# Attention over heads: GpSimd adds the halves of the weighted values of ten heads; the sum, the spread and the output each get a slot of their own

## The chip, the cores and the metric

The kernel runs on one core of a Trainium2 chip. The metric is device time in microseconds of one execution. Before the change three runs took 3179.53, 3181.57 and 3188.43 us (median 3181.57). The engines are called as in the profile: PE (TensorE, with PEld for its weight loads), DVE (VectorE), ACT (ScalarE), POOL (GpSimd) and SP (SyncE).

## The reference, cut to what matters

The program is a decoder of two layers with six parts, on 64 batches of 128 tokens with 128 features in float32. The changed part is the fourth, attention over heads: each token attends, within itself, from each of its 16 heads to each of its 16 heads; a head has 8 features.

```python
def _L1_attn_ref(x, Wq, Wk, Wv, Wo, bo):
    N_HEADS = 16
    N, S, D = x.shape
    H = N_HEADS
    hd = D // H
    q = (x @ Wq.T).reshape(N, S, H, hd).transpose(0, 2, 1, 3)
    k = (x @ Wk.T).reshape(N, S, H, hd).transpose(0, 2, 1, 3)
    v = (x @ Wv.T).reshape(N, S, H, hd).transpose(0, 2, 1, 3)
    att = jnp.einsum('nqhd,nkhd->nhqk', q, k)
    att = jax.nn.softmax(att / jnp.sqrt(jnp.asarray(hd, x.dtype)), axis=3)
    out = jnp.einsum('nhqk,nkhd->nqhd', att, v).reshape(N, S, D)
    return out @ Wo.T + bo
...
x = x + _L1_attn_ref(_layernorm(x, axis=-1), L1_attn_Wq, ...)
```

After the transpose q, k and v are (batch, head, token, feature), while the einsum reads its letters as if token stood before head: so the softmax runs over pairs of heads, separately for each token. The result, (batch, head, token, feature of the head), is reshaped to 128 rows of 128 without a transpose: row 8 h + t // 16 of the output comes from head h and the sixteen tokens of group t // 16. In the kernel a token is a partition, and the scores of one token are a 16 x 16 square in the free dimension.

## The kernel before, in words

The kernel runs its parts one after the other, each as a stage with a barrier at its end. The whole `x` (128 partitions of tokens, 64 batches, 128 features) stays in SBUF. The changed stage is `attention_over_heads`, lines 1455 to 1626. It handles one batch at a time, in a pipeline written out by hand. Time is cut into slots; `run_slots` (lines 52 to 64) gives each engine its own instructions for slot after slot, the first and last slots written out, the middle ones in a loop unrolled by four. In slot t a step with lag n works on batch t - n. There is no planner: an engine carries out the steps in the order in which its function lists them, and waits on semaphores before each.

The steps of one batch, with their lags before the change:

- lag 0 and `TURN` (1): ACT normalizes into `xn` (L1544), PE transposes it (L1515), ACT copies it to `xT` (L1538), POOL adds the output bias to `x` (L1580).
- `PROJECT` (2): PE computes q, k and v (L1520), ACT copies them to `qkv` (L1550).
- `MULTIPLY` (3): POOL multiplies q and k of all 16 x 16 pairs of heads into `qk`, 2048 elements per token (L1575).
- `SCORE` (4): PE adds up the eight features with sixteen matmul instructions against the identity (L1508); DVE takes the maximum (L1613) and subtracts it (L1616); ACT takes the exponential into `ps_e` (L1564).
- `WEIGH` (5): DVE multiplies the weights with v into `ev`, 2048 elements per token (L1597), sums the weights (L1599), takes the reciprocal (L1601), sums `ev` over its last 16 (L1603) and scales to `o` (L1607).
- `SPREAD` (6): ACT writes `o` eight times into `r`, each time scaled by the mask of one group of sixteen tokens (L1557).
- `LAST` (7): PE multiplies with the output weights (L1526), DVE adds to `x` (L1622) and takes statistics (L1624). One slot later, for every fourth batch, POOL computes the scalars of the next normalization for four batches (`scalars_of_four`, lines 171 to 246), a chain of small instructions each of which waits for the one before.

Within a slot the order on each engine is: PE scores, transpose, projection, output; ACT `xT`, `xn`, `qkv`, spread, exponential; POOL `qk`, bias, scalars; DVE weigh (all five instructions), maximum and difference, addition to `x` and statistics. `qkv` has four buffers, `qk`, `dif`, `o`, `r` and `ps_e` two, `ev`, `z` and `rz` one.

Of the kernel before, what the change touches and what calls it, by code (L numbers as in the profile page):

```python
# [18 lines left out]
ALU = mybir.AluOpType  # L19
ACT = mybir.ActivationFunctionType  # L20
AX = mybir.AxisListType

P = 128
D = 128
HEADS = 16
HD = 8
# [40 lines left out]
def wait(eng, sem, value):  # L67

    if not (isinstance(value, int) and value <= 0):
        eng.wait_ge(sem, value)  # L70
# [1384 lines left out]
def attention_over_heads(c):  # L1455
# [3 lines left out]

    nc, B = c.nc, c.B  # L1460
    A = P // HEADS
    ctx, sb, ps, sem = stage_scope(c)
    with ctx:
        xn, xT = sb("xn", [P, 2, D]), sb("xT", [P, 2, P])
        qkv = sb("qkv", [P, UNROLL, 3, HD, HEADS])
        qk = sb("qk", [P, 2, HD, HEADS, HEADS])
        top, dif = sb("top", [P, HEADS]), sb("dif", [P, 2, HEADS, HEADS])
        z, rz = sb("z", [P, HEADS]), sb("rz", [P, HEADS])
        ev = sb("ev", [P, HEADS, HD, HEADS])
        o = sb("o", [P, 2, HEADS, HD])  # L1470
        r = sb("r", [P, 2, HD, HEADS, A])
        ps_x, ps_qkv, ps_y = ps("ps_x"), ps("ps_qkv"), ps("ps_y")
        ps_s = [ps(f"ps_s{i}") for i in range(2)]
        ps_e = [ps(f"ps_e{i}") for i in range(2)]
        names = ("xn_ready", "xT_ps", "xT_ready", "qkv_ps", "qkv_ready", "qk_ready", "s_ps", "top_done", "dif_ready", "exp_done",
                 "z_done", "rz_done", "ev_done", "sums_done", "o_ready", "r_ready", "y_ps", "x_done", "biased")
        (xn_ready, xT_ps, xT_ready, qkv_ps, qkv_ready, qk_ready, s_ps, top_done, dif_ready, exp_done,
         z_done, rz_done, ev_done, sums_done, o_ready, r_ready, y_ps, x_done, biased) = (sem(n) for n in names)
        block = ctx.enter_context(nc.Block())

        TURN, PROJECT, MULTIPLY, SCORE, WEIGH, SPREAD, LAST = 1, 2, 3, 4, 5, 6, 7
        LAG = LAST
        full = [P, HD, HEADS, HEADS]
        final_in = sem("final_in")
# [9 lines left out]
        def weights_of(u):  # L1494
            return ps_e[u % 2][:, 0:HEADS * HEADS].rearrange("p (i j) -> p i j", i=HEADS)

        def sums_of(u):
            return ps_e[u % 2][:, HEADS * HEADS:HEADS * HEADS + D].rearrange("p (i d) -> p i d", i=HEADS)

        @block.tensor  # L1500
        def _(pe):
# [29 lines left out]
        @block.scalar  # L1531
        def _(act):
            def slot(sl):
                if at := sl.step(TURN):
                    s, u = at
                    act.wait_ge(xT_ps, s + 1)
                    wait(act, qkv_ps, s - 1)
                    nc.scalar.activation(xT[:, u % 2, :], ps_x[:, 0:P], ACT.Copy).then_inc(xT_ready, 1)  # L1538
                if at := sl.step(0):
                    s, u = at  # L1540
                    wait(act, xT_ps, s - 1)
                    if sl.fixed and sl.t == MULTIPLY + 1:
                        act.wait_ge(late_rated, 4)
                    nc.scalar.activation(xn[:, u % 2, :], c.x[:, s, :], ACT.Identity, scale=c.rstd[:, bass.ds(s, 1)],  # L1544
                                         bias=c.shift[:, bass.ds(s, 1)]).then_inc(xn_ready, 1)
                if at := sl.step(PROJECT):
                    s, u = at
                    act.wait_ge(qkv_ps, s + 1)
                    wait(act, ev_done, s - 3)
                    nc.scalar.activation(qkv[:, u, :, :, :], ps_qkv[:, 0:3 * D].rearrange("p (n d h) -> p n d h", n=3, h=HEADS),  # L1550
                                         ACT.Copy).then_inc(qkv_ready, 1)
                if at := sl.step(SPREAD):
                    s, u = at
                    act.wait_ge(o_ready, s + 1)
                    wait(act, y_ps, s - 1)
                    for a in range(A):
                        ins = nc.scalar.activation(r[:, u % 2, :, :, a], o[:, u % 2, :, :].rearrange("p h d -> p d h"), ACT.Copy,  # L1557
                                                   scale=c.w["a1_rows"][:, a:a + 1])
                    ins.then_inc(r_ready, 1)
                if at := sl.step(SCORE):  # L1560
                    s, u = at
                    act.wait_ge(dif_ready, s + 1)
                    wait(act, o_ready, s - 1)
                    nc.scalar.activation(weights_of(u), dif[:, u % 2, :, :], ACT.Exp, scale=HD ** -0.5).then_inc(exp_done, 1)  # L1564

            run_slots(act, slot, B, LAG)

        @block.gpsimd
        def _(pool):
            def slot(sl):  # L1570
                if at := sl.step(MULTIPLY):
                    s, u = at
                    pool.wait_ge(qkv_ready, s + 1)
                    wait(pool, s_ps, s - 1)
                    nc.gpsimd.tensor_tensor(qk[:, u % 2, :, :, :], qkv[:, u, 0, :, :].unsqueeze(3).broadcast_to(full),  # L1575
                                            qkv[:, u, 1, :, :].unsqueeze(2).broadcast_to(full), ALU.mult).then_inc(qk_ready, 1)
                if at := sl.step(TURN):
                    s, u = at
                    pool.wait_ge(xn_ready, s + 1)
                    nc.gpsimd.tensor_tensor(c.x[:, s, :], c.x[:, s, :], c.w["a1_b"][:, :], ALU.add).then_inc(biased, 1)  # L1580
                if sl.fixed and sl.t == MULTIPLY:
                    scalars_of_four(c, pool, late_scaled, late_rated, B - 4, four, False, True, 0)
                if (at := sl.step(LAST + 1)) and at[1] % 4 == 3 and not (sl.fixed and at[0] == B - 1):
                    s, u = at
                    pool.wait_ge(stats_done, s + 1)
                    scalars_of_four(c, pool, scaled, rated, s - 3, four, False, True)

            run_slots(pool, slot, B, LAG)

        @block.vector  # L1590
        def _(dve):
            def slot(sl):
                if at := sl.step(WEIGH):
                    s, u = at
                    n = [P, HEADS, HD, HEADS]
                    dve.wait_ge(exp_done, s + 1)
                    nc.vector.tensor_tensor(ev[:, :, :, :], weights_of(u).unsqueeze(2).broadcast_to(n),  # L1597
                                            qkv[:, u, 2, :, :].unsqueeze(1).broadcast_to(n), ALU.mult).then_inc(ev_done, 1)
                    nc.vector.tensor_reduce(z[:, :], weights_of(u), AX.X, ALU.add).then_inc(z_done, 1)  # L1599
                    dve.wait_ge(z_done, s + 1)  # L1600
                    nc.vector.reciprocal(rz[:, :], z[:, :]).then_inc(rz_done, 1)  # L1601
                    dve.wait_ge(ev_done, s + 1)
                    nc.vector.tensor_reduce(sums_of(u), ev[:, :, :, :], AX.X, ALU.add).then_inc(sums_done, 1)  # L1603
                    dve.wait_ge(rz_done, s + 1)
                    dve.wait_ge(sums_done, s + 1)
                    wait(dve, r_ready, s - 1)
                    nc.vector.tensor_tensor(o[:, u % 2, :, :], sums_of(u), rz[:, :].unsqueeze(2).broadcast_to([P, HEADS, HD]),  # L1607
                                            ALU.mult).then_inc(o_ready, 1)
                if at := sl.step(SCORE):
                    s, u = at  # L1610
                    dve.wait_ge(s_ps, s + 1)
                    score = ps_s[u % 2][:, 0:HEADS * HEADS].rearrange("p (i j) -> p i j", i=HEADS)
                    nc.vector.tensor_reduce(top[:, :], score, AX.X, ALU.max).then_inc(top_done, 1)  # L1613
                    dve.wait_ge(top_done, s + 1)
                    wait(dve, exp_done, s - 1)
                    nc.vector.tensor_tensor(dif[:, u % 2, :, :], score, top[:, :].unsqueeze(2).broadcast_to([P, HEADS, HEADS]),  # L1616
                                            ALU.subtract).then_inc(dif_ready, 1)
                if at := sl.step(LAST):
                    s, u = at
                    dve.wait_ge(y_ps, s + 1)  # L1620
                    dve.wait_ge(biased, s + 1)
                    nc.vector.tensor_tensor(c.x[:, s, :], c.x[:, s, :], ps_y[:, 0:D], ALU.add).then_inc(x_done, 1)  # L1622
                    dve.wait_ge(x_done, s + 1)
                    nc.vector.bn_stats(c.stats[:, s, :], c.x[:, s, :]).then_inc(stats_done, 1)  # L1624

            run_slots(dve, slot, B, LAG)


# [1109 lines left out]
```

## Time and profile before

| what | value |
|---|---|
| median of three runs | 3181.57 us |
| profiled execution, its own time | 3173.24 us |
| profiled execution, span of the core | 3171.5 us |
| mean granted TensorE clock over the span | 0.958 |
| busy over the span: PE, PEld, DVE, ACT, POOL | 89%, 73%, 70%, 60%, 57% |
| first `ev` to last `ev` start (64 batches) | 1737.3 to 2169.7 us |

The rows below come from one profiled execution. Rows in order of time show the start and the duration of an instruction or of a run of equal ones ("x16" is sixteen of them), and in brackets the idle time of the engine before it and what ended it. A start-to-start distance can be shorter than a duration, because an engine takes up its next instruction before the last one's end is recorded. Rows of groups show the number of instructions, the busy time of all, and the mean duration in ns.

### The profile page before, as it was taken

How to read it: one execution, taken by the hardware profiler on the slowest of the kernel's cores; microseconds unless marked ns; L12 is line 12 of the kernel's file. 1: busy time of each engine (PE TensorE's matmuls, PEld its weight loads, DVE VectorE, ACT ScalarE, POOL GpSimd, SP SyncE). 2: the span in 40 equal slices, each digit the busy share in tenths (PEclk: the TensorE clock that was granted, in tenths of full speed). 3: DMA queues.
4: the chain of work that ended last, by engine and by line, in shares of the span. 5: the costliest groups of instructions: out<-in, count | busy, mean ns of one | idle time of the engine just before them, and what ended most of it. 6: DMA issues, size and time to landing. Idle time of an engine off the chain costs nothing. (4 is left out here: it accounts for less than half of the span.)

```text
span 3171.5 us, 79074 instructions
## 1 busy us (share of the span) xinstructions
PE 2810.4 (89%) x26182; PEld 2315.9 (73%) x26183; DVE 2213.5 (70%) x4747; ACT 1914.9 (60%) x4303; POOL 1819.8 (57%) x2990
## 2 busy tenths in 40 slices
PE   6999997999999999499995999996789999999996
PEld 4666675888888888387774777774467777777775
DVE  4877885667666676445553999996878787878643
ACT  2555553666666666354442667674677777777762
POOL 3333333556666666425556777773667777777752
PEclk9999998999999999699997999997699999999998
DMA  5555563000000000122222000000000000000000
GB/s 151 156 143 157 157 169 107 2 5 13 14 11 13 13 12 15 68 69 74 74 74 68 1 0 0 0 0 1 1 1 5 8 5 8 5 8 5 8 5 10
DMA packets 205118, 129.51 MB, mean 41 GB/s; under 512 B 14256, under 2 KB 197528, under 8 KB 204184
## 3 DMA queue, kind: packets, MB, share of 16 engines
q1 hardware_dynamic: 196632, 108.60, 12.1%
q0 software_dynamic: 8192, 16.79, 1.7%
q8 instruction: 208, 3.41, 0.4%
q14 instruction: 86, 0.70, 0.1%
HBM read 34.85 MB, written 90.51 MB: 40 GB/s over the span
## 5 line engine op out<-in xcount | busy, mean ns | idle before, releaser
L445 ACT ACTIVATE a_e<-a_ps_s 128x512 f32<-128x512 f32 x256 | 138.9, 595 | 216.9 <-PE a_ps_s L371 216.9
L1575 POOL TENSOR_TENSOR a_qk<-a_qkv 128x2048 f32<-128x2048 f32 x64 | 235.3, 3676 | 57.8 <-ACT a_qkv L1550 53.6
L1508 PE MATMUL a_ps_s<-a_qk,w_ident 128*128 128x256 f32 x1024 | 236.7, 385 | 26.5 <-POOL a_qk L1575 26.4
L988 POOL TENSOR_TENSOR x_p<-x_p,x_rz 128x1232 f32<-128x1232 f32 x64 | 143.9, 2248 | 170.4 <-DVE x_rz L1097 170.4
L1508 PEld LDWEIGHTS a_ps_s<-a_qk,w_ident 128*128 128x128 f32 x1024 | 192.1, 192 | 55.9 <-issue 22.4
L524 POOL TENSOR_TENSOR a_k_bd<-a_kT,w_block 128x512 f32<-128x512 f32 x64 | 67.1, 1050 | 280.2 <-ACT a_kT L476 280.2
L1366 POOL DMA_INDIRECT f_yg<-f_rows_out,f_index x128 | 122.8, 959 | 177.7 <-DVE f_yo L1446 159.3
L547 DVE TENSOR_REDUCE a_nmax<-a_ps_s 128x4 f32<-128x512 f32 x256 | 164.0, 682 | 84.3 <-PE a_ps_s L366 84.3
L1557 ACT ACTIVATE a_r<-a_o,w_a_rows 128x128 f32<-128x128 f32 x512 | 220.8, 522 | 2.1 <-DVE a_o L1607 2.1
L2224 POOL TENSOR_TENSOR x_sq<-x_e 128x1232 f32<-128x1232 f32 x64 | 143.3, 2240 | 127.4 <-DVE x_t_sq L2383 127.3
L1104 DVE TENSOR_REDUCE x_top<-x_ps_s 128x16 f32<-128x1232 f32 x64 | 91.2, 1425 | 110.3 <-PE x_ps_s L728 110.3
L2102 ACT ACTIVATE x_pT<-x_ps_s 77x512 f32<-77x512 f32 x256 | 142.3, 590 | 34.6 <-PE x_ps_s L1979 34.6
L1526 PEld LDWEIGHTS a_ps_y<-w_a_o,a_r 128*128 128x128 f32 x1024 | 123.1, 195 | 54.6 <-issue 36.3
L865 ACT ACTIVATE x_uu_hi<-x_ps_u 128x308 fp32r<-128x308 f32 x256 | 101.7, 423 | 90.6 <-PE x_ps_u L728 90.4
L366 PE MATMUL a_ps_s<-a_k_bd,a_q 32*128 32x128 f32 x2048 | 154.1, 289 | 1.2 <-issue 1.2
L2205 POOL TENSOR_TENSOR x_d<-x_d,x_g 128x1232 f32<-128x1232 f32 x64 | 144.0, 2249 | 18.5 <-ACT x_g L2164 18.5
L1526 PE MATMUL a_ps_y<-w_a_o,a_r 128*128 128x128 f32 x1024 | 131.4, 283 | 24.4 <-DVE x L1622 24.2
L1979 PE MATMUL x_ps_s<-w_ident,x_d 128*77 128x128 f32 x1024 | 145.2, 280 | 7.7 <-DVE x_d L2366 7.6
L1597 DVE TENSOR_TENSOR a_ev<-a_ps_e,a_qkv 128x2048 f32<-128x2048 f32 x64 | 146.0, 2281 | 5.2 <-ACT a_ps_e L1564 4.1
L882 ACT ACTIVATE x_pT<-x_ps_s 77x512 f32<-77x512 f32 x256 | 140.0, 594 | 13.4 <-PE x_ps_s L786 12.0
L1979 PEld LDWEIGHTS x_ps_s<-w_ident,x_d 128*77 128x77 f32 x1024 | 124.4, 152 | 31.2 <-issue 22.1
L1019 POOL DMA_INDIRECT f_rows_in<-f_xr,f_where x120 | 121.1, 1009 | 39.2 <-issue 28.6
(588 smaller groups left out, 9755.6 us busy)
## 6 DMA issues: line engine op xcount, KB each, us to landing
f_rows_in<-a_zeros SPq DMA_DIRECT2D x31, 1088.0 KB, 5.4
f_rows_out<-a_zeros SPq DMA_DIRECT2D x31, 1088.0 KB, 10.2
f_xin<-f_rows_in SPq DMA_DIRECT2D x135, 64.0 KB
f_rows_out<-f_yo SPq DMA_DIRECT2D x135, 64.0 KB
out<-x SPq DMA_DIRECT2D x16, 256.0 KB
f_raw<-in_late_f SPq DMA_DIRECT2D x2, 1408.0 KB, 6.1
w_ctx<-in_ctx SPq DMA_DIRECT2D x1, 2464.0 KB
f_rows_in<-f_xr,f_where POOLq DMA_INDIRECT x128
```

What stands on the lines that cost most here:

```text
L366: nat = nc.tensor.matmul(ps_s[g][:, j * P:j * P + P], q[strip(g), u % 4, :], k_bd[strip(g), u % 4, j, :], start=False, stop=j == GROUP - 1)
L547: nc.vector.tensor_reduce(nmax[:, g, :], ps_s[g][:, :].rearrange("p (t k) -> p t k", t=GROUP), AX.X, ALU.max, negate=True).then_inc(max_do ...
L988: nc.gpsimd.tensor_tensor(wide, wide, rz[:, :].unsqueeze(2).broadcast_to([P, HEADS, K]), ALU.mult).then_inc(p_ready, 1)
L1508: ins = nc.tensor.matmul(ps_s[u % 2][:, 0:HEADS * HEADS], c.ident[:, :], qk[:, u % 2, k, :, :], start=k == 0, stop=k == HD - 1)
L1526: ins = nc.tensor.matmul(ps_y[:, 0:D], r[:, u % 2, k, :, :], c.w["a1_o"][:, k, :], start=k == 0, stop=k == HD - 1)
L1557: ins = nc.scalar.activation(r[:, u % 2, :, :, a], o[:, u % 2, :, :].rearrange("p h d -> p d h"), ACT.Copy, scale=c.w["a1_rows"][:, a:a + 1])
L1575: nc.gpsimd.tensor_tensor(qk[:, u % 2, :, :, :], qkv[:, u, 0, :, :].unsqueeze(3).broadcast_to(full), qkv[:, u, 1, :, :].unsqueeze(2).broad ...
L1597: nc.vector.tensor_tensor(ev[:, :, :, :], weights_of(u).unsqueeze(2).broadcast_to(n), qkv[:, u, 2, :, :].unsqueeze(1).broadcast_to(n), ALU ...
L1979: ins = nc.tensor.transpose(ps_s[0:K, r, j * P:j * P + P], d[:, spread % RING, r, j, :], c.ident[:, :])
L2102: nc.scalar.activation(pT[:, GROUP * r:GROUP * r + GROUP, :], ps_s[0:K, r, :].rearrange("p (j q) -> p j q", j=GROUP), ACT.Copy).then_inc(p ...
L2205: nc.gpsimd.tensor_tensor(wide, wide, g[:, a, b, :].unsqueeze(2).broadcast_to([P, HEADS, K]), ALU.mult).then_inc(dg_ready, 1)
L2224: nc.gpsimd.tensor_tensor(sq[:, :, :], e[:, s % 2, :, :], e[:, s % 2, :, :], ALU.mult).then_inc(sq_ready, 1)
```

## The change

POOL adds, for the first ten heads, the upper eight of each sixteen weighted values to the lower eight, into a new tile `pairs` (640 elements per token). DVE sums the sixteen values for the other six heads, and the eight pair sums for these ten. `WEIGH` is cut in two: the product, the sum of the weights and the reciprocal stay in it; the sums and `o` go to a new step `SUM`, one slot later. `SPREAD` and `LAST` go one slot later too. `ev` and `rz` get two buffers, the sums a PSUM bank of their own. ACT's exponential waits for `ev` and `z` of the batch before instead of `o`. In POOL's order the new add stands between the `qk` product and the bias addition; DVE does `SUM` between `WEIGH` and the maximum.

```diff
+    HALF, FOLDED = HEADS // 2, 10
...
-        z, rz = sb("z", [P, HEADS]), sb("rz", [P, HEADS])
-        ev = sb("ev", [P, HEADS, HD, HEADS])
+        z, rz = sb("z", [P, HEADS]), sb("rz", [P, 2, HEADS])
+        ev = sb("ev", [P, 2, HEADS, HD, HEADS])
+        pairs = sb("pairs", [P, 2, FOLDED, HD, HALF])
...
+        ps_sums = ps("ps_sums")
...
-        TURN, PROJECT, MULTIPLY, SCORE, WEIGH, SPREAD, LAST = 1, 2, 3, 4, 5, 6, 7
+        TURN, PROJECT, MULTIPLY, SCORE, WEIGH, SUM, SPREAD, LAST = 1, 2, 3, 4, 5, 6, 7, 8
...
-        def sums_of(u):
-            return ps_e[u % 2][:, HEADS * HEADS:HEADS * HEADS + D].rearrange("p (i d) -> p i d", i=HEADS)
+        sums = ps_sums[:, 0:D].rearrange("p (i d) -> p i d", i=HEADS)
...
                     act.wait_ge(dif_ready, s + 1)
-                    wait(act, o_ready, s - 1)
+                    wait(act, ev_done, s - 1)
+                    wait(act, z_done, s - 1)
...
+                if at := sl.step(WEIGH):
+                    s, u = at
+                    pool.wait_ge(ev_done, s + 1)
+                    wait(pool, sums_done, 2 * (s - 1))
+                    nc.gpsimd.tensor_tensor(pairs[:, u % 2, :, :, :], ev[:, u % 2, 0:FOLDED, :, 0:HALF], ev[:, u % 2, 0:FOLDED, :, HALF:HEADS],
+                                            ALU.add).then_inc(paired, 1)
...
                     dve.wait_ge(exp_done, s + 1)
-                    nc.vector.tensor_tensor(ev[:, :, :, :], weights_of(u).unsqueeze(2).broadcast_to(n),
+                    wait(dve, paired, s - 1)
+                    nc.vector.tensor_tensor(ev[:, u % 2, :, :, :], weights_of(u).unsqueeze(2).broadcast_to(n),
...
-                    nc.vector.reciprocal(rz[:, :], z[:, :]).then_inc(rz_done, 1)
+                    nc.vector.reciprocal(rz[:, u % 2, :], z[:, :]).then_inc(rz_done, 1)
+                if at := sl.step(SUM):
+                    s, u = at
                     dve.wait_ge(ev_done, s + 1)
-                    nc.vector.tensor_reduce(sums_of(u), ev[:, :, :, :], AX.X, ALU.add).then_inc(sums_done, 1)
+                    nc.vector.tensor_reduce(sums[:, FOLDED:HEADS, :], ev[:, u % 2, FOLDED:HEADS, :, :], AX.X, ALU.add).then_inc(sums_done, 1)
+                    dve.wait_ge(paired, s + 1)
+                    nc.vector.tensor_reduce(sums[:, 0:FOLDED, :], pairs[:, u % 2, :, :, :], AX.X, ALU.add).then_inc(sums_done, 1)
                     dve.wait_ge(rz_done, s + 1)
-                    dve.wait_ge(sums_done, s + 1)
+                    dve.wait_ge(sums_done, 2 * (s + 1))
                     wait(dve, r_ready, s - 1)
-                    nc.vector.tensor_tensor(o[:, u % 2, :, :], sums_of(u), rz[:, :].unsqueeze(2).broadcast_to([P, HEADS, HD]),
+                    nc.vector.tensor_tensor(o[:, u % 2, :, :], sums, rz[:, u % 2, :].unsqueeze(2).broadcast_to([P, HEADS, HD]),
                                             ALU.mult).then_inc(o_ready, 1)
```

## Rows read from the trace of the kernel before

**Rows 1.** The page: busy time, share of the span and instructions of each engine.
```profile
PE 2810.4 (89%) x26182; PEld 2315.9 (73%) x26183; DVE 2213.5 (70%) x4747; ACT 1914.9 (60%) x4303; POOL 1819.8 (57%) x2990
```
**Rows 2.** Busy time by stretch, the stage's middle; after the engines PEclk, DMA, GB/s.
```profile
1900.00:2000.00 100.00, 91.84 (x518) 77.20 (x517) 94.48 (x133) 68.79 (x174) 72.82 (x81) 1.00 0.00 0
```
**Rows 3.** Order of time, DVE, one batch: start, duration, engine, line, operation.
```profile
2012.84 2.27 DVE L1597 TENSOR_TENSOR a_ev<-a_ps_e,a_qkv 128x2048 f32<-128x2048 f32 x1
2015.03 0.41 DVE L1599 TENSOR_REDUCE a_z<-a_ps_e 128x16 f32<-128x256 f32 x1
...
2015.65 2.24 DVE L1603 TENSOR_REDUCE a_ps_e<-a_ev 128x128 f32<-128x2048 f32 x1
2017.98 0.29 DVE L1607 TENSOR_TENSOR a_o<-a_ps_e,a_rz 128x128 f32<-128x128 f32 x1
...
2019.61 2.27 DVE L1597 TENSOR_TENSOR a_ev<-a_ps_e,a_qkv 128x2048 f32<-128x2048 f32 x1
```
**Rows 4.** Order of time, POOL, around one chain of scalars.
```profile
1971.86 0.20 POOL L207 TENSOR_TENSOR a_four<-stats 128x4 f32 x1 [2.15 <-DVE stats L1624]
...
1977.78 3.67 POOL L1575 TENSOR_TENSOR a_qk<-a_qkv 128x2048 f32<-128x2048 f32 x1 [0.32 <-issue]
...
1981.41 0.45 POOL L1580 TENSOR_TENSOR x<-x,w_a_b 128x128 f32 x1
...
1981.83 3.67 POOL L1575 TENSOR_TENSOR a_qk<-a_qkv 128x2048 f32<-128x2048 f32 x1
```
**Rows 5.** Order of time, PE, around the scores behind a chain.
```profile
1954.14 3.72 PE L1508 MATMUL a_ps_s<-a_qk,w_ident 128*128 128x256 f32 x16 [1.58 <-POOL a_qk L1575]
...
1981.58 3.71 PE L1508 MATMUL a_ps_s<-a_qk,w_ident 128*128 128x256 f32 x16 [1.57 <-POOL a_qk L1575]
...
1985.24 0.81 PE L1520 MATMUL a_ps_qkv<-w_a_qkv,a_xT 128*128 128x384 f32 x2
...
1987.67 3.62 PE L1508 MATMUL a_ps_s<-a_qk,w_ident 128*128 128x256 f32 x16
```
**Rows 6.** Groups by line and shape, POOL, whole span: count, busy, mean ns.
```profile
L524 POOL TENSOR_TENSOR a_k_bd<-a_kT,w_block 128x512 f32<-128x512 f32 x64 | 67.1, 1050 | 280.2 <-ACT a_kT L476 280.2
...
L2232 POOL TENSOR_TENSOR x_full<-x_full,f_row_f2b 128x512 f32<-128x512 f32 x16 | 20.3, 1268 | 1.3
...
L975 POOL COPY x_raw<-w_ctx 128x308 f32 x10 | 4.5, 452 | 0.0
```
**Rows 7.** Order of time, ACT, in the slot behind a chain.
```profile
1986.17 0.49 ACT L1550 ACTIVATE a_qkv<-a_ps_qkv 128x384 f32<-128x384 f32 x1
1986.56 3.46 ACT L1557 ACTIVATE a_r<-a_o,w_a_rows 128x128 f32<-128x128 f32 x8
```
**Rows 8.** Order of time, all engines: an exponential and the `ev` behind it.
```profile
1964.20 0.39 ACT L1564 ACTIVATE a_ps_e<-a_dif 128x256 f32<-128x256 f32 x1 [1.64 <-DVE a_dif L1616]
...
1964.72 2.27 DVE L1597 TENSOR_TENSOR a_ev<-a_ps_e,a_qkv 128x2048 f32<-128x2048 f32 x1
```
**Rows 9.** Order of time, PE, matmuls behind idle time, at the stage's ends.
```profile
1738.20 5.41 PE L1508 MATMUL a_ps_s<-a_qk,w_ident 128*128 128x256 f32 x16 [3.19 <-POOL a_qk L1575]
...
2162.85 2.02 PE L1526 MATMUL a_ps_y<-w_a_o,a_r 128*128 128x128 f32 x16 [1.21 <-DVE x L1622]
2169.54 3.49 PE L1526 MATMUL a_ps_y<-w_a_o,a_r 128*128 128x128 f32 x16 [4.67 <-DVE x L1622]
2175.44 3.21 PE L1526 MATMUL a_ps_y<-w_a_o,a_r 128*128 128x128 f32 x16 [2.41 <-DVE x L1622]
```
**Rows 10.** Busy time by stretch, one microsecond within the first of these.
```profile
1740.00:1741.00 1.00, 1.00 (x4) 0.77 (x3) 1.00 (x2) 0.00 (x0) 1.00 (x1) 0.50 0.00 0
```
**Rows 11.** Order of time, DVE: first `ev`, last `ev`, last instruction of the stage.
```profile
1737.27 2.29 DVE L1597 TENSOR_TENSOR a_ev<-a_ps_e,a_qkv 128x2048 f32<-128x2048 f32 x1 [2.09 <-ACT a_ps_e L1564]
...
2169.65 2.29 DVE L1597 TENSOR_TENSOR a_ev<-a_ps_e,a_qkv 128x2048 f32<-128x2048 f32 x1
...
2181.66 0.29 DVE L1624 BATCH_NORM_STATS2 stats<-x 128x6 f32<-128x128 f32 x1
```

More of the change, by code:

```diff
@@ L1474, in attention_over_heads @@
         ps_e = [ps(f"ps_e{i}") for i in range(2)]
-        names = ("xn_ready", "xT_ps", "xT_ready", "qkv_ps", "qkv_ready", "qk_ready", "s_ps", "top_done", "dif_ready", "exp_done",
+        ps_sums = ps("ps_sums")
+        names = ("paired", "xn_ready", "xT_ps", "xT_ready", "qkv_ps", "qkv_ready", "qk_ready", "s_ps", "top_done", "dif_ready", "exp_done",
                  "z_done", "rz_done", "ev_done", "sums_done", "o_ready", "r_ready", "y_ps", "x_done", "biased")
-        (xn_ready, xT_ps, xT_ready, qkv_ps, qkv_ready, qk_ready, s_ps, top_done, dif_ready, exp_done,
+        (paired, xn_ready, xT_ps, xT_ready, qkv_ps, qkv_ready, qk_ready, s_ps, top_done, dif_ready, exp_done,
          z_done, rz_done, ev_done, sums_done, o_ready, r_ready, y_ps, x_done, biased) = (sem(n) for n in names)
         block = ctx.enter_context(nc.Block())
-        TURN, PROJECT, MULTIPLY, SCORE, WEIGH, SPREAD, LAST = 1, 2, 3, 4, 5, 6, 7
+        TURN, PROJECT, MULTIPLY, SCORE, WEIGH, SUM, SPREAD, LAST = 1, 2, 3, 4, 5, 6, 7, 8
         LAG = LAST
```

## The prediction

> **What bounds the kernel now.** I read the engine totals first: no engine is full over the whole span (PE 89%, DVE 70%, POOL 57%) [rows 1], so the changed stage has to be read by itself. It is attention over heads, from about 1725 to 2182 us. In the table by stretch its middle shows DVE busy 94.5 of 100 us, PE 91.8, POOL 72.8, ACT 68.8, with TensorE at its full clock [rows 2]. DVE bounds it. Next I read DVE in order of time: one batch from `ev` to the next `ev` takes 2019.61 - 2012.84 = 6.77 us without a gap, 2.33 us of it the sum over 16 values (start of the sum to start of `o`) [rows 3]. Then GpSimd: every fourth slot it runs the chain of small instructions for the scalars of four batches (5.92 us from L207 to the next `qk`); a `qk` and the bias add take 4.05 us together [rows 4]. Last PE: the score matmuls that come behind that chain start 27.44 us after their predecessors four slots before [rows 5]. So the beat of the stage is four slots in 27.44 us, 4 x 6.77 = 27.1 of them DVE.
>
> **The change, part by part.** *What DVE loses.* The one sum of 2048 elements becomes one of 768 (six heads) and one of 640 (ten heads, already halved). From the sums of 2048 in 2.24 us and of 256 in 0.41 us an element costs 1.02 ns and an instruction about 0.15 [rows 3]: 0.93 + 0.80 = 1.73 instead of 2.24, so DVE's slot falls to about 6.2 us. That is a gain only if nothing else sets the beat.
>
> *What GpSimd gains.* One add per batch, 64 in all, 640 elements with two different inputs. No row has 640. The nearest is the add of 512 elements with two full inputs, 1268 ns; the bias add of 128 took 0.45 [rows 4, 6]. That is 2.12 ns an element, so 1.54 us, or 1.50 to the start of the next. Bounds: the product with one broadcast operand, 512 in 1.05 us [rows 6], gives 1.30; the copy with one input, 308 in 0.45 us, scaled to 640 gives 0.94; the upper end is 1.75, if each element cost a sixth more than the dearest row. I take 1.50, by the nearest row (an add with two full inputs).
> GpSimd's needs in four slots before: 4 x 4.05 + 5.92 = 22.1 us, so it has 5.3 us free of 27.44. Four adds need 6.0. **The cover is too small**: by its own work alone the beat becomes 28.1 us. Part of its spare time is a wait of 2.15 us for the statistics before L207 [rows 4]; the rest it waits for `qkv`.
> The Trainium skill, Perfetto Trace Analysis, "GPSIMD Engine Instruction", says that a GpSimd span in a profile isn't to be relied on and should be timed from start to start. By that the add is 1.50 and not 1.54, which over 64 is under 3 us; the sum above goes by starts already.
>
> *The wait that it adds.* GpSimd's order in a slot is `qk`, add, bias add, and at every fourth the chain. The add waits for `ev` of the same slot, and behind it in the queue stand the chain and the next `qk`, for which PE's scores wait. Let a `qk` behind a chain end at 0. From there, in this kernel's rows: scores start at 0.13 (1981.45 to 1981.58); PE works a whole slot, 6.09 (1981.58 to 1987.67); from the next scores to the end of the projection 4.47 (1981.58 to 1986.05) [rows 5]; ACT copies `qkv` and starts the spread after 0.12 + 0.39, and the eight spread instructions take 3.46 [rows 7]. `exp` is queued behind them, 0.39, then 0.13 until `ev` starts [rows 8], and 2.28 until it ends [rows 3]. Sum 17.46 us: that is when the add of the third slot on can start. GpSimd by its own work would be there at 3 x (1.50 + 0.41 + 3.63) = 16.6. It waits 0.8 us, and then: add 1.50, bias 0.41, chain 5.92, `qk` 3.67. The beat is 17.46 + 11.50 = **28.96 us**. With the add at 0.94 this loop would still give 28.4.
>
> *What becomes of PE.* Its four slots take 4 x 6.09 = 24.4 us, and all of its idle time falls in one piece, in front of the scores behind the chain: 4.5 us instead of 1.57 [rows 5]. What such a hole does is to be seen at the stage's ends [rows 9]. After an idle 3.19 us sixteen score matmuls took 5.41 us instead of 3.62 [rows 5]; after 4.67 and 2.41 us the sixteen output matmuls took 3.49 and 3.21 instead of 2.02 after 1.21. The granted clock was 0.50 in such a piece (1.2 instead of 2.4 GHz) [rows 10]. After 1.57 us nothing of the kind is seen [rows 5]. So I expect the clock to fall once per beat, at a price of 1.2 to 1.8 us; I take 1.5. The scores so slowed stand at the head of the loop above, so the price is paid in full: **30.46 us** a beat.
> The Trainium skill, TensorE: Matmul & The Clock Gate, "Why this matters for your kernels", warns of TensorE idle gaps between bursts, after which the clock goes back to half. The rows above agree. If the rule did not bite here, the beat would stay at 28.96 us.
>
> *Two buffers, `rz` by two, own bank, exp's new waits.* `exp` now waits for `ev` and `z` of the batch before, both over when DVE has made its `dif`: nothing. The second `ev` buffer and the separate PSUM bank cost no instruction; at most they lengthen no wait. *One slot more of lag*: below, at the end.
>
> **The sum**, against the profiled execution (span 3171.5). First `ev` at 1737.3 as before [rows 11]. GpSimd isn't yet full in the seven slots up to the first chain in the loop (slots 5 to 12): PE's pace of 6.1 and 2 us of start, so `ev` of slot 12 at 1782. Its end, add, bias, chain, `qk`: + 2.3 + 1.5 + 0.4 + 5.9 + 3.7 = 1796. There are 14 chains (slots 12 to 64), so 13 full beats: 13 x 30.46 = 396, 2192. From there to the last `ev`: add 1.5, then PE's and DVE's last slots, 11.1 by DVE's pace, and once more 1.5 for the clock: 14.1, 2206. From the last `ev` to the end of the last statistics 12.3 us before [rows 11]; now the wait for the add and the slot more put two spreads (7 us) one behind the other: 15.2. End of the stage 2221.3 instead of 2182.0 [rows 11]: **+39.3 us**. What follows the stage (fed by a barrier) is unchanged. The span becomes 3210.8. The profiled execution took 3173.2 by its own time, the median shown is 3181.57, 8.3 above it; the difference put on the median gives **3221**.
>
> **Rivals.**
> *B, the clock holds.* Same loop, but TensorE stays at full clock through a 4.5 us hole. For it: in the stage's middle the clock never left 1.00 [rows 2]. Against: three holes out of three of 2.4 us and more were followed by slow matmuls [rows 9]. 14 x 1.5 = 21 less: +18.3, 3200.
> *C, GpSimd's work alone.* The add finds `ev` ready always, the clock fall is absorbed. Beat 28.1: 13 x 0.86 less than B: +7, 3189. Against: `exp` is queued behind the spread [rows 7, 8], which I can't see shortened. This is also the most that a cheap add can make of the loop (0.94 gives a beat of 28.4).
> *D, faster.* One mechanism: GpSimd does the adds in the time that it now idles in front of L1575 and L207. It decides where four adds fit 5.3 us, at 1.33 us an add, and where `ev` is early enough not to be waited for. At 0.94 GpSimd would need 25.9 a beat, against 4 x 6.2 = 24.8 of DVE: 13 x 1.6 = 21 less, and 5 less at the ends: 3155. For it: the products with a broadcast operand are that cheap or nearly. Against: every add with two full inputs is dearer, and the loop.
> *E, dearer.* The add at 1.75 and register work of the added waits showing in the chain: 14 x 1.3 = 18 more, 3239.
>
> **How the numbers follow.** Own case 0.57, with its range 3208 to 3232 (the price of the clock, 14 x 0.3 either way, and of the add, 14 x 0.25 x 1 up or down, and a few us between runs). B 0.17, C 0.11, D 0.08, E 0.07. The range reaches down to C's middle and up to just short of E: 3187 to 3235, leaving out D, half of C and most of E. A measurement of this kernel can tell 0.3%, 9.5 us, from no change. Slower by more: own case, B, E and a share of C, 0.82; within: 0.10; faster: D, 0.08.
>
> **What would show it.** Right: POOL above 90% busy in the stage's middle, DVE near 85%; `pairs` add about 1.5 us; a wait of GpSimd for `ev` once in four slots; scores behind a chain 30 us apart, idle over 4 us before them, 5.2 us long instead of 3.7, and granted clock about 0.9 in the stage. The two sums 0.93 and 0.80 us. Wrong: the add under 1.3 us; beats under 28; the clock at 1.00 in the stage (then B or C); DVE still above 90%.

## The result, and the profile after

| kernel | median, us | runs |
|---|---|---|
| before | 3180.55 | 4 |
| after | 3226.86 | 4 |
| ratio | 1.0138, 95% interval 1.0113 to 1.0164 | |

The kernel became slower by 1.38%, 36 to 52 us; 3221 was forecast. The profiled execution took 3228.11 us, span 3226.3, 54.8 longer than before. From the first `ev` to the first matmul of the next stage the changed stage took 486.3 us (1749.63 to 2235.95), before 445.6 (1737.27 to 2182.85): **+40.7**, and +39.3 was forecast. The part ahead of the stage, whose code is the same, was 12.4 us longer in this execution (over the profiles of the experiments the first `ev` starts anywhere from 1712 to 1747 us), the part behind it 1.7. So I compare stages by their own length, and programs by the ratios of medians.

Busy time by engine over the span, after; the counterpart before is in [rows 1]:
```profile
PE 2840.5 (88%) x26182; PEld 2350.6 (73%) x26183; DVE 2179.5 (68%) x4811; ACT 1922.2 (60%) x4303; POOL 1918.5 (59%) x3054
```
Here the reader sees nearly nothing: DVE gave up 34 us, POOL took on 99, and PE, whose work didn't change, is busy 30 us longer. The stage's middle, by stretch as in [rows 2] (behind the five engines stand the granted TensorE clock, DMA, GB/s):
```profile
1900.00:2000.00 100.00, 86.63 (x459) 74.29 (x458) 74.85 (x128) 61.25 (x154) 86.09 (x90) 0.90 0.00 0
```
DVE went from 94.5 to 74.9 us of 100, POOL from 72.8 to 86.1, and no engine is full. A beat that got longer with no engine full is a loop of waits, or work that is slow while it counts as busy; here it is both. What the changed instructions cost, after, in groups (count, busy, mean ns, idle time before them and what ended it), and who waits for whom in the stage (us in total, times, longest):
```profile
L1510 PE MATMUL a_ps_s<-a_qk,w_ident 128*128 128x256 f32 x1024 | 265.7, 419 | 68.4 <-POOL a_qk L1578 68.4
L1607 DVE TENSOR_TENSOR a_ev<-a_ps_e,a_qkv 128x2048 f32<-128x2048 f32 x64 | 146.2, 2284 | 26.5 <-ACT a_ps_e L1567 24.1 <-issue 2.4
L1584 POOL TENSOR_TENSOR a_pairs<-a_ev 128x640 f32<-128x640 f32 x64 | 98.4, 1538 | 48.8 <-DVE a_ev L1607 48.8
L1615 DVE TENSOR_REDUCE a_ps_sums<-a_ev 128x48 f32<-128x768 f32 x64 | 57.8, 903 | 0.0
L1617 DVE TENSOR_REDUCE a_ps_sums<-a_pairs 128x80 f32<-128x640 f32 x64 | 51.9, 811 | 0.0
```
```profile
PE a_ps_s L1510 <- POOL a_qk L1578: 54.0, 12, 4.9
POOL a_pairs L1584 <- DVE a_ev L1607: 32.5, 22, 2.3
```
The add is 1.54 us and the sums 0.90 and 0.81: the prices are as forecast (1.54, 0.93, 0.80). PE waits twelve times, 4.5 us each, for the `qk` behind a chain. In order of time, PE's score matmuls (start, duration, idle before and what ended it), to be set beside [rows 5]:
```profile
1929.10 5.96 PE L1510 MATMUL a_ps_s<-a_qk,w_ident 128*128 128x256 f32 x16 [4.46 <-POOL a_qk L1578]
1937.44 3.62 PE L1510 MATMUL a_ps_s<-a_qk,w_ident 128*128 128x256 f32 x16
...
1960.05 5.85 PE L1510 MATMUL a_ps_s<-a_qk,w_ident 128*128 128x256 f32 x16 [4.46 <-POOL a_qk L1578]
...
1990.89 5.41 PE L1510 MATMUL a_ps_s<-a_qk,w_ident 128*128 128x256 f32 x16 [4.46 <-POOL a_qk L1578]
...
2021.28 5.95 PE L1510 MATMUL a_ps_s<-a_qk,w_ident 128*128 128x256 f32 x16 [4.46 <-POOL a_qk L1578]
```
The beats are 30.95, 30.84 and 30.39 us, and the short one is the one that begins with the short scores (5.41). POOL in order of time through one beat, to be set beside [rows 4]:
```profile
1956.33 3.67 POOL L1578 TENSOR_TENSOR a_qk<-a_qkv 128x2048 f32<-128x2048 f32 x1
...
1967.38 3.67 POOL L1578 TENSOR_TENSOR a_qk<-a_qkv 128x2048 f32<-128x2048 f32 x1
1973.27 1.56 POOL L1584 TENSOR_TENSOR a_pairs<-a_ev 128x640 f32<-128x640 f32 x1 [2.22 <-DVE a_ev L1607]
...
1979.67 1.55 POOL L1584 TENSOR_TENSOR a_pairs<-a_ev 128x640 f32<-128x640 f32 x1 [0.79 <-DVE a_ev L1607]
1981.17 0.46 POOL L1589 TENSOR_TENSOR x<-x,w_a_b 128x128 f32 x1
1981.58 0.21 POOL L207 TENSOR_TENSOR a_four<-stats 128x4 f32 x1
...
1987.16 3.67 POOL L1578 TENSOR_TENSOR a_qk<-a_qkv 128x2048 f32<-128x2048 f32 x1
```
POOL waits for `ev` in the third and fourth slot of the beat, then does add, bias, chain and `qk` one behind the other (11.16 us from 1979.67 to the end of `qk`), while PE waits. The granted clock around the hole (the hole, the first 4 us of scores, the 2 us after):
```profile
1955.50:1960.00 4.50, 0.09 (x1) 0.00 (x0) 4.29 (x8) 2.62 (x7) 4.18 (x5) 0.73 0.00 0
1960.00:1962.00 2.00, 1.95 (x5) 1.59 (x6) 1.97 (x4) 0.00 (x0) 2.00 (x3) 0.50 0.00 0
1962.00:1964.00 2.00, 2.00 (x6) 1.60 (x5) 1.41 (x3) 0.00 (x0) 2.00 (x1) 0.50 0.00 0
1964.00:1966.00 2.00, 2.00 (x10) 1.69 (x9) 0.07 (x1) 0.00 (x0) 2.00 (x2) 0.90 0.00 0
```
The clock falls inside the hole and stays at 0.50, 1.2 GHz, for the first four microseconds of scores: 5 or 6 matmuls in 2 us, against 10 and more later.

### The profile page after: what moved, and what is told of

Same layout as the page of the kernel before. It is cut to its first block and busy times, and to the rows that moved or that the text cites. A ratio compares the mean times of both kernels' runs of the same rounds, so it can differ in the third digit from the quotient of the medians.

```text
span 3226.3 us, 79417 instructions
## 1 busy us (share of the span) xinstructions
PE 2840.5 (88%) x26182; PEld 2350.6 (73%) x26183; DVE 2179.5 (68%) x4811; ACT 1922.2 (60%) x4303; POOL 1918.5 (59%) x3054
## 5 line engine op out<-in xcount | busy, mean ns | idle before, releaser
L1510 PE MATMUL a_ps_s<-a_qk,w_ident 128*128 128x256 f32 x1024 | 265.7, 419 | 68.4 <-POOL a_qk L1578 68.4
L1510 PEld LDWEIGHTS a_ps_s<-a_qk,w_ident 128*128 128x128 f32 x1024 | 212.5, 213 | 106.9 <-POOL a_qk L1578 74.2
L1019 POOL DMA_INDIRECT f_rows_in<-f_xr,f_where x120 | 121.4, 1012 | 39.0 <-issue 28.1
L1305 PE MATMUL f_ps_y<-f_w,f_aT 128*128 x810 | 123.0, 289 | 22.8 <-DVE f_yo L1446 19.7
```

The source lines that it names most:

```text
L1510: ins = nc.tensor.matmul(ps_s[u % 2][:, 0:HEADS * HEADS], c.ident[:, :], qk[:, u % 2, k, :, :], start=k == 0, stop=k == HD - 1)
```

## The experiments

My theory after the result: the new wait for `ev` of the same slot, with the chain behind it in POOL's queue, closes a loop of 28.7 us, and the clock fall adds about 2.2 us to it. Rivals: POOL's work alone (C), and the clock as a consequence that costs nothing. Ratios are to the kernel before in runs on the same chip, with 95% intervals; "stage" is first `ev` to the next stage's first matmul, set against 445.6; it is of the one profiled execution, which can lie some us off the median. A beat is four slots, scores behind a chain to the next such scores.

### The add alone, without and with its wait

The kernel before, with one more POOL add of 640 elements per batch, on a tile of ones (`still`) that nothing else touches; DVE's work is unchanged. The second kernel has the marked line too.
```diff
+                if at := sl.step(WEIGH):
+                    s, u = at
+                    wait(pool, padded, s - 1)
+                    pool.wait_ge(ev_done, s + 1)      # the second kernel only
+                    nc.gpsimd.tensor_tensor(pairs[:, u % 2, :, :, :], still[:, :, :, 0:HEADS // 2], still[:, :, :, HEADS // 2:HEADS], ALU.add).then_inc(padded, 1)
```
Without the wait:

> The kernel before, with an add of 640 elements of a constant tile in every slot of GpSimd, in the place of the new add, its result unused; it waits for nothing of DVE's. Theory (most of the loss is the wait for ev and what it sets off): GpSimd's own work makes the beat 28.1 us, so +5 to +24 us, about 3190, with GpSimd never waiting for DVE in mid-stage. Rival (the load of the add on GpSimd by itself is the loss): as slow as the changed kernel, 3220 or more.

With the wait:

> As the one with the constant add, but the add waits for ev of its slot, as the new add does; DVE still sums all 2048 elements. Theory: the loop closes, with DVE's longer slot (6.77 instead of 6.2 us) in it: beat about 31.6 us, +50 us, about 3234, so at least 25 us slower than the one without the wait. Rival (the load alone): the same time as without the wait, within 8 us.

Measured without it: ratio 1.0030 (1.0018 to 1.0042), 3188.39 us, stage 454.6, +9.0; a beat of 28.1. With it: 1.0191 (1.0169 to 1.0214), 3237.51 us, stage 503.4, +57.8. The times are as expected (about 3190 and 3234). PE's scores behind the chain, without the wait:
```profile
1910.79 5.40 PE L1511 MATMUL a_ps_s<-a_qk,w_ident 128*128 128x256 f32 x16 [3.84 <-POOL a_qk L1581]
1938.85 5.40 PE L1511 MATMUL a_ps_s<-a_qk,w_ident 128*128 128x256 f32 x16 [2.13 <-POOL a_qk L1581]
1966.93 3.72 PE L1511 MATMUL a_ps_s<-a_qk,w_ident 128*128 128x256 f32 x16 [2.14 <-POOL a_qk L1581]
1995.03 3.72 PE L1511 MATMUL a_ps_s<-a_qk,w_ident 128*128 128x256 f32 x16 [3.04 <-POOL a_qk L1581]
```
The reader sees slow and full-clock scores, and the same beat of 28.06 to 28.10 behind either: while POOL's own work bounds the stage, the clock fall is free. With the wait, of what POOL waited for:
```profile
POOL a_pairs L1587 <- DVE a_ev L1608: 31.8, 20, 2.3
```
The wait with what it sets off, the fall of the clock included, and not the add's 1.5 us, makes +49 of the +58. Here DVE still has its whole sum in the slot, so this loop is longer than that of the changed kernel.

### The clock kept up

The changed kernel, with extra matmuls into columns of PSUM that nobody reads, in the last slot of the beat: the hole is filled, the loop stays. First 13 calls, then 9.
```diff
+                    if u == 1:
+                        pe.wait_ge(xT_ready, min(s + LAST, B) if sl.fixed else s + LAST)
+                        for _ in range(13):      # 9 in the second kernel
+                            nc.tensor.matmul(ps_x[:, P:3 * P], c.ident[:, :], c.w["a1_qkv"][:, 0:2 * P], start=True, stop=True)
```
13 calls:

> The changed kernel, with 13 more matmuls of 256 columns on PE behind the output matmuls of the slot after each chain of scalars, into columns of PSUM that nobody reads (work that the result doesn't need). They fill about 3 of the 4.5 us in which PE waits for the products. Theory (wait loop and clock): the clock stays at 1.00, the scores behind a chain take 3.7 us again instead of 5.4 to 6.2, the beat of four slots falls from 30.9 to about 28.9 us, the time by 14 x 2.1 = 29 us to about 3198. Rival (the clock fall is absorbed somewhere, GpSimd's work or its wait alone makes the time): less than 5 us off the changed kernel's 3227.

9 calls:

> As the kernel with 13 added matmuls, with 9 of them: 13 ran 5.8 us and held the scores behind them back by 1.06 us in each beat (29.6 us a beat, clock 1.00); 9 should run 4.0 us and end before the products are there. Theory (wait loop, and the clock's price on it): clock 1.00, beat 28.5 to 29.0 us, 14 x 2.1 = 29 us off the changed kernel: about 3198. Rival (the 9 us that 13 matmuls gained were all there is to the clock): 3217.

13 calls: 1.0113 (1.0090 to 1.0137), 3217.53 us, stage 481.2. That missed (3198 was expected): the fillers took 5.78 us, not 3, and overran the hole. Each call is two matmuls in the trace (x26), where I had reckoned with one. `qk` ended at 1955.79, the scores started 1.06 later:
```profile
1951.24 5.78 PE L1533 MATMUL a_ps_x<-w_a_qkv,w_ident 128*128 128x256 f32 x26
...
1952.12 3.67 POOL L1582 TENSOR_TENSOR a_qk<-a_qkv 128x2048 f32<-128x2048 f32 x1
...
1956.85 3.62 PE L1510 MATMUL a_ps_s<-a_qk,w_ident 128*128 128x256 f32 x16
```
9 calls: 1.0055 (1.0036 to 1.0073), 3167.47 us against 3148.08, +19.4; stage 464.5, +18.9; rival B gave +18.3 for a kept clock. PE, the window, and POOL's one wait of the beat:
```profile
1922.23 3.72 PE L1510 MATMUL a_ps_s<-a_qk,w_ident 128*128 128x256 f32 x16 [0.56 <-POOL a_qk L1582]
1950.92 3.72 PE L1510 MATMUL a_ps_s<-a_qk,w_ident 128*128 128x256 f32 x16 [0.55 <-POOL a_qk L1582]
```
```profile
1900.00:2000.00 100.00, 98.35 (x555) 85.49 (x554) 83.02 (x140) 69.12 (x173) 91.13 (x97) 1.00 0.00 0
```
```profile
1939.73 1.55 POOL L1588 TENSOR_TENSOR a_pairs<-a_ev 128x640 f32<-128x640 f32 x1 [0.80 <-DVE a_ev L1611]
```
Clock 1.00, beat 28.69, one wait of 0.80 us: this is the loop of the prediction (28.96, one wait of 0.8) laid bare. With it the beats of the changed kernel come out within 0.02 us: scores of 5.41 instead of 3.72 give 28.69 + 1.69 = 30.38 (measured 30.39), of 5.96 give 30.93 (30.95), of 5.85 give 30.82 (30.84). The clock's part is thus shown: 486.3 - 464.5 = 22 us of the stage, from one profiled execution of each, on different chips.

### A short add in the same place

`FOLDED` 2 instead of 10 in the changed kernel: POOL's load nearly as before, the waits the same, DVE's sums longer.
```diff
-    HALF, FOLDED = HEADS // 2, 10
+    HALF, FOLDED = HEADS // 2, 2
```

> The changed kernel with 2 heads folded instead of 10: the add is 128 elements (0.45 instead of 1.54 us), DVE sums 14 heads over 16. GpSimd's own work is then 23.7 us a beat, under the 27.4 of before. Theory (the wait for ev with the chain behind it closes the loop whatever the add costs): beat 30.9 - 1.1 (add) + 0.4 (DVE's longer slot) = 30.2 us, clock still falling, about 3216. Rival (GpSimd's load is the cause): no slower than before, 3180 or less.

Measured 1.0145 (1.0117 to 1.0174), 3194.90 us against 3148.08, +46.8; stage 489.2.
```profile
1924.12 6.30 PE L1510 MATMUL a_ps_s<-a_qk,w_ident 128*128 128x256 f32 x16 [3.88 <-POOL a_qk L1578]
1954.83 6.31 PE L1510 MATMUL a_ps_s<-a_qk,w_ident 128*128 128x256 f32 x16 [3.88 <-POOL a_qk L1578]
```
```profile
1900.00:2000.00 100.00, 88.36 (x471) 75.93 (x470) 82.14 (x128) 64.00 (x162) 69.74 (x87) 0.90 0.00 0
```
The add takes 0.45 us, POOL is busy 70 of 100, and the loss is as large as with ten heads. A smaller piece of work does not help when it waits in the same place. The loss was 12 us above what I expected. Part of that is the clock: the scores took 6.3 instead of 3.72, 2.6 a beat where I had 2.1, and the beat is 30.71 instead of 30.2, some 7 us in all; the rest is open.

### What opens the loop

Three edits of the changed kernel, each at another place of the loop. The chain cut into four parts, one a slot:
```diff
-                if (at := sl.step(LAST + 1)) and at[1] % 4 == 3 and not (sl.fixed and at[0] == B - 1):
...
-                    scalars_of_four(c, pool, scaled, rated, s - 3, four, False, True)
+                for part in range(4):
+                    if (at := sl.step(LAST + 1 + part)) and at[1] % 4 == 3 and not (sl.fixed and at[0] == B - 1):
...
+                        scalars_of(c, pool, scaled, rated, s - 3, 4, four, False, True, s - 3, parts=(part,))
```

> The changed kernel, with the chain of scalars cut into its four parts, one per slot, instead of all four in every fourth slot. Nothing is left out. Theory: no slot of GpSimd is longer than about 7.7 us, so PE has no hole over 2.4 us, the clock stays at 1.00, the wait loop over three slots (17.5 us) is shorter than three slots, and GpSimd's own work of 28.1 to 28.5 us sets the beat: about 3188, 39 us under the changed kernel. Rival (load alone): no change against 3227.

ACT's exponential ahead of the spread (the block of `SCORE` moved up, nothing else):
```diff
+                if at := sl.step(SCORE):
...
                 if at := sl.step(SPREAD):
...
-                if at := sl.step(SCORE):
```

> The changed kernel, with ACT taking the exponential of a slot before the eight spread instructions instead of behind them. Theory (the spread, 3.46 us, stands in the wait loop in front of exp): the exponential behind late scores starts with the difference, and what then sets ev is DVE in its own order, which waits for PE's output matmuls: the loop shortens by about 2 us a beat, from 30.9 to about 29 us, 14 x 2 = 28 us off, about +19 us over the kernel before. Rival (the spread isn't on the path): no change, +47 us over before.

POOL's add one slot later, `ev` and `rz` with four buffers:
```diff
-        TURN, PROJECT, MULTIPLY, SCORE, WEIGH, SUM, SPREAD, LAST = 1, 2, 3, 4, 5, 6, 7, 8
+        TURN, PROJECT, MULTIPLY, SCORE, WEIGH, HALVE, SUM, SPREAD, LAST = 1, 2, 3, 4, 5, 6, 7, 8, 9
...
-                if at := sl.step(WEIGH):
+                if at := sl.step(HALVE):
...
```

> The changed kernel, with GpSimd's add one slot later than ev (a step of its own between WEIGH and SUM, four buffers of ev and rz, one more slot of lag): all work stays, and the add finds its ev ready. Theory (the wait for ev of the same slot is the loss above GpSimd's load): GpSimd never waits in mid-stage, beat 28.1 us as with the constant add, the clock may fall behind the chain but at no price: +9 us of the constant add and 3 us for one slot more at the end, about +12 us over the kernel before. Rival (the load or the clock is the loss, whatever waits): above +30 us.

| edit | median, us | before | ratio (95%) | stage | beat | clock | POOL of 100 |
|---|---|---|---|---|---|---|---|
| chain in four | 3180.83 | 3179.65 | 1.0007 (0.9991 to 1.0022) | 448.2 | 27.98 | 1.00, 1.00 | 93.1 |
| exp first | 3185.22 | 3177.73 | 1.0027 (1.0015 to 1.0038) | 458.6 | 27.7 to 30.1 | 0.98, 0.93 | 91.3 |
| add a slot later | 3190.14 | 3177.73 | 1.0038 (1.0025 to 1.0052) | 450.9 | 27.7 to 29.1 | 0.93, 0.95 | 92.1 |

The clock is given for 1900 to 2000 and 2000 to 2100 us, the busy time of POOL for the first of these. With the clock up all three have beats of 27.7 to 28.0 us, about what POOL's own work needs: four times 5.54 from one `qk` to the next (1961.84 to 1967.38 in the changed kernel) and a chain of 5.58 make 27.7. In two of them the clock still falls in some beats. "Add a slot later" came out as expected, and its scores show that such a fall is mostly free there:
```profile
2022.12 5.41 PE L1510 MATMUL a_ps_s<-a_qk,w_ident 128*128 128x256 f32 x16 [1.83 <-POOL a_qk L1578]
2049.89 3.72 PE L1510 MATMUL a_ps_s<-a_qk,w_ident 128*128 128x256 f32 x16 [1.83 <-POOL a_qk L1578]
```
The beat behind the slow scores is 27.77 us, and the one behind the others 27.73 (to 2077.62). Only two slower runs of scores, 6.41 and 6.71 us, made beats of 28.77 and 29.07.

"Exp first" does more than I expected (+7.5 us, not +19). In its trace the exponential starts ahead of the spread and no longer behind it:
```profile
1963.80 0.39 ACT L1559 ACTIVATE a_ps_e<-a_dif 128x256 f32<-128x256 f32 x1 [1.79 <-DVE a_dif L1630]
1964.12 3.43 ACT L1565 ACTIVATE a_r<-a_o,w_a_rows 128x128 f32<-128x128 f32 x8
```
It opens the loop only while the clock is up. Behind slow scores POOL waits for `ev` again, eight times from 1800 to 2150 us, and the beat is longer:
```profile
1885.87 6.75 PE L1510 MATMUL a_ps_s<-a_qk,w_ident 128*128 128x256 f32 x16 [2.74 <-POOL a_qk L1578]
...
1915.97 5.37 PE L1510 MATMUL a_ps_s<-a_qk,w_ident 128*128 128x256 f32 x16 [2.08 <-POOL a_qk L1578]
...
1944.69 3.72 PE L1510 MATMUL a_ps_s<-a_qk,w_ident 128*128 128x256 f32 x16 [2.10 <-POOL a_qk L1578]
```
```profile
POOL a_pairs L1584 <- DVE a_ev L1607: 6.4, 8, 0.8
```
The beats are 30.10 and 28.72 us; less what the scores took above 3.72, both give a loop of 27.07. I had expected 29 us a beat, the clock's price in every one. Here only six of the thirteen beats from 1801.66 to 2170.54 us began with slow scores, and the mean beat is 28.4.

"Chain in four" was 7 us better than expected, and the only one of the three with the clock at 1.00 throughout, since it spreads PE's idle time over the slots. Two of its scores, the second of them the longest idle of its beat:
```profile
1890.41 3.72 PE L1510 MATMUL a_ps_s<-a_qk,w_ident 128*128 128x256 f32 x16 [0.40 <-POOL a_qk L1578]
...
1911.74 3.72 PE L1510 MATMUL a_ps_s<-a_qk,w_ident 128*128 128x256 f32 x16 [1.51 <-POOL a_qk L1578]
```

### The chain cut in the kernel before

The same cut, without the add: does the chain cost the kernel before anything?

> The kernel before with the chain cut into its four parts, one per slot; nothing else changed. Theory: DVE bounds it, its 6.77 us a slot stay, only the late scores behind the chain go (27.44 to 27.1 us a beat): -5 us, about 3175. Rival (the chain in one piece is what costs, folding or not): 3160 or less.

No gain is measured where I expected 5 us: 1.0000 (0.9984 to 1.0015), 3151.48 us, stage 443.6. The beat is the same 27.44:
```profile
1912.05 3.62 PE L1508 MATMUL a_ps_s<-a_qk,w_ident 128*128 128x256 f32 x16
...
1939.49 3.62 PE L1508 MATMUL a_ps_s<-a_qk,w_ident 128*128 128x256 f32 x16
```
I had read the 0.36 us of a beat above 4 x 6.77 as the price of the late scores. It is there without them: two neighbouring slots of each four take 6.95 and 6.97 us from `ev` to `ev`, and the other two 6.76. Its cause stays open.

### A better version

With the chain cut, POOL's load is what remains, and it falls with the heads that it folds. 6 heads, and 5:

> The changed kernel with the chain cut into four parts, one per slot, and 6 heads folded instead of 10. The cut chain with 10 heads had a beat of 27.98 us, set by GpSimd. The add of 384 elements costs 0.54 us less: GpSimd needs 25.8, DVE 4 x 6.34 = 25.4, PE 24.4. Theory: beat about 26.1 us, clock 1.00, 15 x 1.3 + 5 = 24 us under before: about 3157. Rival (GpSimd's load has nothing to do with it once the wait is gone): the 3181 of the cut chain with 10 heads.

> The chain cut into four parts and 5 heads folded. With 6 the beat was 25.83 us, GpSimd 92% and DVE 95% busy, so the balance is near. Theory: GpSimd 4 x 0.14 us less, DVE 4 x 0.07 us more; if DVE (25.6 + 0.3 + the 0.36 us that a turn of its loop costs) is the bound already, the beat is 26.1 and the time 3 us over that with 6 heads; if GpSimd is, 25.3 and 8 us under it. I expect the first: 0.992 to 0.994 of the kernel before.

6 heads: 0.9913 (0.9886 to 0.9939), 3123.59 us against 3148.08, -24.5, stage 421.8, as expected. The same kernel on another chip (its expectation: 

> The kernel with the cut chain and 6 heads folded once more, on the chip of this call and beside the one with 5: again 24 us under the kernel before, 0.992 of it.

) gave 0.9932 (0.9917 to 0.9948), 3155.68 against 3177.73, stage 423.5. 5 heads gave 0.9942 (0.9927 to 0.9958), 3156.97, stage 428.0, with a beat of 26.1 as the expectation had it for DVE as the bound. The intervals overlap, so 5 and 6 heads are not told apart. With 6:
```profile
1921.79 3.72 PE L1510 MATMUL a_ps_s<-a_qk,w_ident 128*128 128x256 f32 x16 [0.98 <-POOL a_qk L1578]
1947.62 3.72 PE L1510 MATMUL a_ps_s<-a_qk,w_ident 128*128 128x256 f32 x16 [0.98 <-POOL a_qk L1578]
```
```profile
1900.00:2000.00 100.00, 95.47 (x546) 82.67 (x545) 95.15 (x155) 76.89 (x191) 92.30 (x110) 1.00 0.00 0
```
A beat of 25.83 us, with PE, DVE and POOL all above 92 of 100. It beats both kernels.

## Why the prediction was right, step by step

**DVE.** Forecast sums 0.93 + 0.80 and a slot of 6.2 us; measured 0.90 + 0.81, and 6.10 between two starts of `ev` without a gap (1983.41 to 1989.50). Right, and worth nothing, as DVE no longer sets the beat.

**POOL's load.** 28.1 us a beat was forecast; the add alone, without a wait, gave 28.06 to 28.10. Rival C as a term is right (+7 forecast, +9.0 shown); as an end it was not reached. In the changed kernel's own code the load is nearer 27.7, for the chain is shorter than I took it.

**The loop.** Forecast 17.46 + 11.50 = 28.96 with one wait of 0.8. With the clock kept it is 28.69 with one wait of 0.80. The 0.27 are the chain, from L207 to `qk`: 5.55 in that kernel (5.58 in the changed one, 1981.58 to 1987.16) instead of 5.92, as the row that I took it from had an idle 0.32 before `qk` [rows 4]. The way to the add took 0.1 more, 17.55.

**The hole and the clock.** Hole forecast 4.5, measured 4.46; clock forecast about 0.9, measured 0.90. The price was the mis-sized term: 1.5 a beat with 1.8 as its upper end, measured 1.69 to 2.52, mean 2.09 over the eleven slowed scores from 1805.65 to 2113.59 (5.41 to 6.24 long, where 5.2 was forecast). My bounds came from runs of matmuls in [rows 9] of which the dearest cost 1.8.

**The sum.** In the profile after: from the first `ev` to the first slow scores 56.0 (forecast 58.8), 13 beats 399.6, 30.74 each (396, 30.46), from there to the last `ev` 14.5 (14.0), to the end of the last statistics 15.3 (15.2). The clock's +0.6 and the loop's -0.3 a beat partly cancel, and the start takes 3 back. So the total is closer than its terms, and that part is luck. Rival E was priced too high: a dearer add stands in the loop once, 0.25 a beat, and nothing in the prediction gives the rest of its 1.3.

**What I said would show it.** Scores 30 us apart with over 4 us idle before them, and the add at 1.5, came true. Wrong were three details: POOL is 84 to 86% busy and not above 90, DVE 75 to 77% and not 85, and POOL waits in two slots of four, 2.22 and 0.79 us. The last is an oversight: I put the clock's price on the loop but didn't carry it into the other rows. The slow scores delay `ev` of the first batch too, so POOL waits one slot earlier as well. The two shares were wrong by my own rows. I had set POOL's 28.1 us, with the gaps inside the chain, against the beat, while the profile counts busy time: 72.8% of 27.44 is 20.0 before [rows 2], and with the adds 26.0 of 30.46 is 85%. DVE's 94.5% of 27.44 is 25.9; less four times 0.67 (6.77 to 6.10) it is 76% of 30.46.
The Trainium skill, TensorE: Matmul & The Clock Gate, "Why this matters for your kernels", warns of such idle gaps. It holds for the 4.5 us hole here. Holes of 1.8 to 3.7 us went either way in these runs, and in the kernel with the add and no wait a fall that is off the loop costs nothing.

**How the +40.7 us splits.** POOL's load +9.0 (the add alone); the wait that closes the loop +9.9 more (18.9 with the clock kept); the clock +22. Each is measured, though on different chips and in kernels that differ in DVE's work, so a few us of each may belong to another. The load's share may be the smaller one: with the add a slot later, where all of the change's work is there, the stage is 5.3 longer.

## What to carry to other kernels

Before work is handed to an engine that has time to spare, look at what stands behind it in that engine's queue, and follow the loop: a wait for something of the same slot, ahead of a long serial chain, cost more than the work itself, and an add of 0.45 us in the same place cost as much as one of 1.54. Put the handed-over piece where its input is a slot old, or break up the chain; only then choose how much to hand over by load. And when a loop leaves TensorE idle in one piece of some microseconds, add the clock's fall to the loop, not beside it.

## What the runs showed of the hardware

Whether a hole drops the clock isn't told by its length alone: in the kernel with the add and no wait the scores took 5.40 us after 2.13 us idle, and 3.72 after 2.14, 3.04 and even 3.70. In the kernel with the add a slot later they took 5.41 six times and 3.72 twice after 1.82 to 1.84 us idle. In no kernel here were they slow after 1.74 us idle or less, and from 3.84 on they always were. The price for the same hole differed too: 5.41, 5.85 or 5.96 us after 4.46 idle. Nine calls, 4 us of matmuls that nobody needs, bought 22 us of the stage (26 us by the ratios, 1.0138 to 1.0055); thirteen, 5.8 us, gave most of it away again.
